# Twelve expert tile pairs moved into the first scan group, with loads that wait for a counted number of scattered columns

## The chip, the cores and the metric

The kernel runs on one core of a Trainium2 chip. Its time is the device time of one execution in microseconds. Engine names in the profile: PE is TensorE (PEld its weight loads), DVE is VectorE, ACT is ScalarE, POOL is GpSimd, SP is the engine whose queue issues most DMAs.

## What is computed

`x` is 2 sequences of 512 tokens with 256 features. Both branches read the layer norm of it, and the output is their sum with `x`:

```python
x = L0_attn_hidden_states
xn = _layernorm(x, axis=-1)
x = x + attn_ref(xn, ...) + ffn_ref(xn, ...)

# attn_ref: a selective state space layer, d_inner 512, d_state 16, dt_rank 128
x, z = split(xn @ in_proj_w.T)
x = silu(causal_conv4(x) + conv_b)
dt, Bm, Cm = split(x @ x_proj_w.T)
dt = softplus(dt @ dt_proj_w.T + 2 * dt_proj_b)
# for each channel d and state n, along the 512 tokens:
h[l] = exp(dt[l] * A[d, n]) * h[l - 1] + dt[l] * Bm[l, n] * x[l]
y = sum_n(h * Cm[:, n]) + x * D
out = (y * z) @ out_proj_w.T

# ffn_ref: 64 experts, each token goes to its 8 most probable ones
probs = softmax(xn @ gate_w.T)
out = sum over the 8 chosen e of probs[e] * ((silu(xn @ g_e.T) * (xn @ u_e.T)) @ w2_e.T)
```

## The kernel before

**Experts.** Routing gives each of the 1024 x 8 choices of an expert a slot. Slots are ordered by expert, each expert filled up to whole tiles of 128. There are 128 tiles, taken as 64 pairs (`PAIRS`). GpSimd writes the rows of the normed x to their slots in DRAM (`slot_x`), with one indirect DMA for each of 8 token tiles `t` and 8 slot columns `k` (L327 to L331); `k8` holds a token's slots with the largest first. For each pair SP loads 256 rows of `slot_x` (`load_x`) and two experts' weights (`load_w`, 2 x 384 KB), and stores the result to `slot_y` (`store_y`). TensorE's `step` for pair p is a pipeline of three: `fetch` transposes x of pair p, `gate_up` works on pair p - 1, `down` on pair p - 2. ScalarE copies x and y out of PSUM (`take_x`, `take_y`) and makes the tanh, VectorE has two operations a pair (`hidden`, L592 and L595). `take_y` waits until the store of two pairs before has landed. At the end GpSimd gathers the rows back by 64 indirect DMAs (L371), and they are weighted by `c8` and added: by TensorE with diagonal matrices (`combine`) for seven token tiles, by VectorE in 8 operations for the last (L697).

**Scan.** The 1024 (sequence, channel) rows are 8 groups of 128 partitions, each with 16 states, 128 scans of 512 tokens. For each state ScalarE makes dA (`decay`), someone makes dbu (`spread_u`), VectorE scans (L572) and multiplies by C (`times_c`, L578), and the products are summed in a PSUM bank by matmuls with the identity. `finish_group` closes a group two states into the next.

**Order.** All of it is written out by hand, each engine with its own program:

- Group 0: VectorE alone makes dbu, in `pair0`; the products go to 16 buffers, so it waits for no sum. GpSimd issues the scatters meanwhile. SP then waits for all scatters and 12 sums before it loads x.
- Groups 1 to 5 (`G1` to before `G2`): scans and expert pairs interleaved, a light group with 12 pairs (`LIGHT`), group 3 (`GH`) heavy with 16, where also the rows of B and C of the second sequence are spread through PSUM. GpSimd makes dbu here (L337) and adds the products in pairs (L344), so TensorE has 8 sums a group.
- Groups 6 and 7 (`G2`, `G3`): `pair0` on VectorE again, with the gathers on GpSimd and `combine` and `project_out` on TensorE.

```python
            sp.wait_ge(scat, 16 * NT * K)
            sp.wait_ge(acc_ok, 3 * PART + C)
            for i in range(4):
                load_x(i, i)
```

## Time and profile before

| | us |
|---|---|
| median of 3 runs | 508.83 (508.74 to 509.46) |
| the profiled execution | 509.57 |
| its span, first to last instruction | 507.4 |
| VectorE busy | 430.5 |
| TensorE busy | 430.4 |
| GpSimd busy | 293.8 |
| ScalarE busy | 246.7 |

The profiled execution took 2.17 us more than its span, and the median of the runs is 0.74 us below it. Busy time is a mean over stages: a stage is best cut where a scan group starts, which is where VectorE's scan reads `dA` and not a PSUM bank (or, in groups that read `dA` throughout, at the first of 16).

### The profile page before, as it was taken

What the parts mean: (1) busy time and instruction counts of PE and PEld (TensorE: products, weight loads), DVE (VectorE), ACT (ScalarE), POOL (GpSimd) and SP (SyncE); (2) the same over time, 40 slices, a digit from 0 to 9 for tenths busy, and PEclk for the clock granted to TensorE, in tenths of its full rate; (3) what the DMA queues carried; (4) which work ended last, traced back from release to release, by engine and by line L of the source; (5) the groups of instructions that cost most, each with busy time, mean ns of one, the idle gap of its engine ahead of it and who ended that gap; (6) DMA issues with size and microseconds to landing.
All of it is one profiled execution on the core that took longest, in us unless ns stands there. A gap on an engine that the chain in (4) does not pass through costs nothing.

```text
span 507.4 us, 9083 instructions
## 1 busy us (share of the span) xinstructions
PE 430.4 (85%) x2136; PEld 304.8 (60%) x2136; DVE 430.5 (85%) x646; ACT 246.7 (49%) x469; POOL 293.8 (58%) x260
## 2 busy tenths in 40 slices
PE   1986969038889999999999997999999949887996
PEld 1732424011157888788787885788878835454754
DVE  5288999989989888898789795888888889999994
ACT  1245367032435655555455665565555632454560
POOL 2000678777756766666545434566766537777772
PEclk9989979655569999999999997999999989997999
DMA  8999399722249999999999997899999944333432
GB/s 278 428 427 424 126 381 398 268 94 103 103 135 310 314 330 348 333 316 314 317 324 312 324 322 268 257 319 326 327 329 331 327 152 122 103 115 106 124 105 88
DMA packets 55417, 132.29 MB, mean 261 GB/s; under 512 B 7616, under 2 KB 11712, under 8 KB 53344
## 3 DMA queue, kind: packets, MB, share of 16 engines
q1 hardware_dynamic: 49248, 115.21, 65.6%
q0 software_dynamic: 6144, 16.79, 10.3%
q8 instruction: 11, 0.18, 0.1%
q14 instruction: 14, 0.11, 0.1%
HBM read 88.39 MB, written 43.58 MB: 260 GB/s over the span
## 4 chain that ended last, share of the span: by engine, by line
SPq 26%; POOL 18%; PE 15%; issue 15%; DVE 12%; DMA 12%; ACT 1%; POOLq 1%; DVEq 0%; ACTq 0%
POOL slot_x L329 13%; SPq L260 10%; SPq L261 6%; DMA slot_x<-bc 5%; DVE bank L572 5%; DMA slot_y<-x_sb 5%; PE bank L1004 4%; SPq L236 4%; SPq L264 3%; SPq L267 3%; PE bank L1015 2%; PE bank L1031 2%; DVE dbu L565 2%; PE bank L974 2%; DVE hc L578 2%
## 5 line engine op out<-in xcount | busy, mean ns | idle before, releaser
L337 POOL TENSOR_TENSOR dbu<-dtu,bc 128x512 f32 x80 | 101.9, 1274 | 99.5 <-DVE bank L572 86.8
L329 POOL DMA_INDIRECT slot_x<-x_sb,slot x64 | 68.8, 1075 | 68.2 <-DMA slot_x<-bc 49.0
L572 DVE TENSOR_TENSOR_SCAN bank<-dA,dbu 128x512 f32<-128x512 f32 x68 | 90.1, 1325 | 10.4 <-POOL dbu L337 1.7
L756 ACT ACTIVATE dA<-dt_sb,a_neg 128x512 f32<-128x512 f32 (+1 forms) x68 | 49.4, 727 | 66.3 <-DVE bank L572 66.1
L572 DVE TENSOR_TENSOR_SCAN bank<-bank,dbu 128x512 f32<-128x512 f32 x60 | 73.8, 1230 | 5.8
L782 ACT COPY x_sb<-bank 128x512 f32<-128x512 f32 x66 | 38.6, 585 | 75.0 <-DMA slot_y<-x_sb 72.7
L1004 PE MATMUL bank<-x_sb,wring 128*128 128x128 f32 x528 | 67.9, 283 | 0.1
L1004 PEld LDWEIGHTS bank<-x_sb,wring 128*128 128x128 f32 x528 | 64.8, 199 | 1.1 <-issue 0.5
L578 DVE TENSOR_TENSOR hc<-bank,bc 128x512 f32<-128x512 f32 x90 | 61.8, 686 | 1.4 <-POOL hp L344 0.3
L756 ACT ACTIVATE bank<-dt_sb,a_neg 128x512 f32 x60 | 41.7, 695 | 9.6 <-DVE bank L572 9.6
L592 DVE SCALAR_TENSOR_TENSOR gt<-th,bank 128x256 f32<-128x256 f32 x65 | 27.0, 416 | 22.5 <-ACT th L776 22.1
L770 ACT COPY x_sb<-bank 128x512 f32<-128x512 f32 x64 | 38.0, 593 | 7.6 <-PE bank L991 7.6
L776 ACT ACTIVATE th<-bank 128x256 f32<-128x256 f32 x65 | 25.2, 388 | 25.4 <-PE bank L1004 24.7
L1015 PE MATMUL bank<-wring,wdt 128*128 128x256 f32 x136 | 35.7, 385 | 1.1 <-ACT x_sb L782 1.0
L974 PE MATMUL bank<-wring,ident 128*128 128x512 f32 x20 | 16.7, 928 | 22.6 <-DVE wring L578 22.6
L344 POOL TENSOR_TENSOR mask<-hc 128x512 f32<-128x512 f32 x21 | 31.2, 1486 | 7.6 <-DVE hc L578 6.4
L595 DVE SCALAR_TENSOR_TENSOR wdt<-gt,bank 128x256 f32<-128x256 f32 x65 | 27.4, 422 | 6.8
L565 DVE TENSOR_TENSOR dbu<-dtu,bc 128x512 f32<-128x512 f32 x48 | 32.4, 674 | 0.5 <-DVEq L559 0.5
L1004 PE MATMUL bank<-x_sb,win 128*128 128x128 f32 x256 | 31.5, 276 | 0.3 <-DMA win<-w_moe 0.3
L1004 PE MATMUL bank<-x_sb,xT 128*128 128x128 f32 x256 | 31.2, 275 | 0.0
L1004 PEld LDWEIGHTS bank<-x_sb,win 128*128 128x128 f32 x256 | 29.9, 192 | 0.5 <-DMA win<-w_moe 0.5
L1004 PEld LDWEIGHTS bank<-x_sb,xT 128*128 128x128 f32 x256 | 29.9, 192 | 0.0
(180 smaller groups left out, 796.5 us busy)
## 6 DMA issues: line engine op xcount, KB each, us to landing
wring<-w_moe SPq DMA_DIRECT2D x64, 384.0 KB, 4.5
slot_y<-x_sb SPq DMA_DIRECT2D x66, 256.0 KB, 4.8
slot_x<-bc SPq DMA_DIRECT2D x16, 1024.0 KB, 22.1
xT<-w_moe SPq DMA_DIRECT2D x32, 384.0 KB, 4.5
win<-w_moe SPq DMA_DIRECT2D x32, 384.0 KB, 4.7
bc<-bc_dram SPq DMA_DIRECT2D x8, 1024.0 KB, 15.9
xg<-slot_x SPq DMA_DIRECT2D x32, 256.0 KB, 4.6
xT<-slot_x SPq DMA_DIRECT2D x16, 256.0 KB, 4.9
```

What stands on the lines that cost most here:

```text
L260: e = sp.value_load(tile_e[0:1, bass.ds(2 * p + j, 1)], min_val=0, max_val=E - 1)
L329: pool.indirect_dma_start(slot_x, bass.IndirectOffsetOnAxis(ap=slot[:, t * K + k:t * K + k + 1], axis=0), x_sb[:, t, :], None).then_inc(sc ...
L337: nc.gpsimd.tensor_tensor(dbu[:, j], at(dtu, g), bc[:, bass.ds(n, 1), 0].rearrange("p a l -> p (a l)"), ALU.mult).then_inc(dbu_ok, 1)
L344: nc.gpsimd.tensor_tensor(hps[j], hc[:, 0], hc[:, 1], ALU.add).then_inc(hp_ok, 1)
L565: nc.vector.tensor_tensor(dbu[:, j], at(dtu, g), bc[:, bass.ds(n, 1), 0].rearrange("p a l -> p (a l)"), ALU.mult).then_inc(dbv_ok, 1)
L572: nc.vector.tensor_tensor_scan(H[:], dA[:, j] if fall is None else fall, dbu[:, j], 0.0, ALU.mult, ALU.add).then_inc(scan_ok, 1)
L578: nc.vector.tensor_tensor(ring[n % len(ring)] if ring else hc[:, j], H[:], bc[:, bass.ds(n, 1), 1].rearrange("p a l -> p (a l)"), ALU.mult ...
L756: nc.scalar.activation(dA[:, j] if fall is None else fall, at(dt_sb, g), ACT.Exp, scale=a_neg[:, bass.ds(g, 1), bass.ds(n, 1)].rearrange(" ...
L770: nc.scalar.copy(xTs[:, i].rearrange("p b d -> p (b d)"), XT[:]).then_inc(xc_ok, 1)
L782: nc.scalar.copy(ysb[:, i].rearrange("p b d -> p (b d)"), YT[:]).then_inc(yc_ok, 1)
L1004: mm = nc.tensor.matmul(GU[1 - i % 2][:, (2 * half + j) * P:(2 * half + j + 1) * P], w_buf[w][:, k * 2 * P + half * P:k * 2 * P + (half + ...
L1015: mm = nc.tensor.matmul(YT[:, j * DM:(j + 1) * DM], hh[:, 2 * (i % 2) + j], w_buf[(2 * i + 4) % 8 + j][:, WGU:], start=True, stop=True)
```

## The change

- Scatters go column by column, lowest slots first (k = 7 first). Each column has a semaphore; GpSimd waits for a column in the middle of the next one and raises `cols_ok`.
- How many columns a pair needs is counted: the smallest slot of each column (`low`, a transpose on TensorE, `lowest`) against the end of the pair (`lim`, `reach`), summed by a matmul to `need`, for the first 16 pairs. SP reads the number and waits for so many columns (`load_early`).
- Group 0 has 12 steps of pairs now. VectorE's `first(n)` has the operations of `hidden` from state 4 on, dbu by VectorE as before. TensorE sums every state by itself (one sum a step, three in step 0). The ring of products is 7 buffers, not 16, and the buffers for x transposed and y no longer lie in `x_sb` but in `wx`/`wgate` (`wxg`) and `wout`.
- Groups 1, 2 light, 3 heavy, 4 light; groups 5, 6 and 7 (`GT` on) are of the last kind. `combine` begins with state 12 of these 48 and does all eight token tiles; VectorE only copies the last two from PSUM.
- `x_sb` is loaded again behind pair 11's loads and not after the last pair; `wout` is loaded after the last store and not after the zeroing.
- ScalarE copies z of groups 4 to 7 ahead of the scans, and its decays run up to five states ahead; GpSimd waits for the sums of group 0 before it makes dbu for group 1.

```diff
-        hc_first = whole + [wdt[:], xg[:, 0].rearrange("p j d -> p (j d)"), xg[:, 1].rearrange("p j d -> p (j d)"),
-                            wx[:].rearrange("p t n -> p (t n)")[:, 0:L]] + [
-            f[:].rearrange("p t e -> p (t e)") for f in (mask, prob, key)] + [hp[:], hc[:, 0], hc[:, 1]]
+        hc_first = [hc[:, 0], hc[:, 1]] + [f[:].rearrange("p t e -> p (t e)") for f in (prob, key)] + [dA[:, 1]] + hps[::-1]
...
+        RING0, AHEAD0, LAST = len(hc_first), 4, 3 * NS
         LIGHT = 3 * QG // 2
-        V_HEAVY, V_LAST = (GH - G1) * LIGHT, (GH - G1) * LIGHT + 2 * QG
-        assert V_LAST + (G2 - GH - 1) * LIGHT == PAIRS
+        V_HEAVY, V_LAST = GH * LIGHT, GH * LIGHT + 2 * QG
+        assert V_LAST + (GT - GH - 1) * LIGHT == PAIRS and NS - AHEAD0 == LIGHT and LIGHT + 4 == EARLY
...
+        PROJ = {8: (4, 0), 10: (5, 0), 20: (4, 1), 22: (5, 1), 24: (6, 0), 26: (7, 0), 28: (6, 1), 30: (7, 1),
+                37: (4, 2), 39: (5, 2), 41: (6, 2), 43: (7, 2)}
+        COMB = 12
...
-            sp.dma_start(wout[:], w_out.rearrange("(t p) n -> p t n", p=P)).then_inc(ld_wout, 16)
...
+            def load_early(p):
+
+                c = sp.value_load(need[0:1, p:p + 1], min_val=1, max_val=K)
+                sp.wait_ge(cols_ok, c)
+                load_x(p, p % 4)
...
-            sp.wait_ge(scat, 16 * NT * K)
-            sp.wait_ge(acc_ok, 3 * PART + C)
-            for i in range(4):
-                load_x(i, i)
+            sp.wait_ge(rt, RT_NEED)
+            sp.wait_ge(c8_ok, NT // 2)
+            for p in range(4):
+                load_early(p)
+            sp.wait_ge(sp_v, SP_STEPS * G)
+
+            for p in range(LIGHT):
+                sp.wait_ge(ye_ok, p + 1 + C)
+                load_w(p + 2, (p + 2) % 4)
+                sp.wait_ge(yc_ok, p + 1 + C)
+                store_y(p, p % 2)
+                sp.wait_ge(t_ok, p + 1)
+                load_early(p + 4)
+            sp.wait_ge(cols_ok, K)
+            sp.dma_start(x_sb[:], x_t).then_inc(ld_res, 16)
...
-            sp.wait_ge(gu_ok, PAIRS + 1 + C)
             for j in range(2):
                 sp.wait_ge(y_st[j], 16 * (PAIRS // 2 + 1) + 16)
-            sp.dma_start(x_sb[:], x_t).then_inc(ld_res, 16)
+            sp.dma_start(wout[:], w_out.rearrange("(t p) n -> p t n", p=P)).then_inc(ld_wout, 16)
...
-            for t in range(NT):
-                for k in range(K):
+
+            def arrived(c):
+
+                pool.wait_ge(scat[c], 16 * NT)
+                pool.sem_inc(cols_ok, 1)
+
+            for c in range(K):
+                k = K - 1 - c
+                for t in range(NT):
+                    if c and t == NT // 2:
+                        arrived(c - 1)
                     pool.indirect_dma_start(
                         slot_x, bass.IndirectOffsetOnAxis(ap=slot[:, t * K + k:t * K + k + 1], axis=0),
-                        x_sb[:, t, :], None).then_inc(scat, 16)
-
+                        x_sb[:, t, :], None).then_inc(scat[c], 16)
+            arrived(K - 1)
+            pool.wait_ge(acc_ok, NS - 2 + C)
...
+            nc.vector.tensor_reduce(low[:], k8[:].rearrange("p t k -> p k t"), AX.X, ALU.min).then_inc(rt, 1)
             dve.wait_ge(pe_r, 5)
             nc.vector.tensor_scalar(tile_e[:], PS[4][0:1, P:P + TILES], float(E - 1), None, ALU.min).then_inc(rt, 1)
-            for d in range(1, DT):
-                conv_block(d)
+            conv_block(1)
+            conv_block(2)
+            dve.wait_ge(pe_r, 6)
+            nc.vector.tensor_reduce(lowest[:], PS[4][0:K, 2 * P:3 * P], AX.X, ALU.min).then_inc(rt, 1)
+            dve.wait_ge(rt, RT_LOWEST)
+            nc.vector.tensor_scalar(reach[:], lim[:], lowest[:], None, ALU.is_ge).then_inc(rt, 1)
+            conv_block(3)
...
+            dve.wait_ge(pe_r, 7)
+            nc.vector.tensor_copy(need[:], PS[4][0:1, 3 * P:3 * P + EARLY]).then_inc(rt, 1)
...
-            for q in range(NS // 4):
-                dve.wait_ge(bc_ld[q], 32)
-                if q == 0:
+                    times_c(g, n, j, hc_end)
+
+            def first(n):
+
+                if n % 4 == 0:
+                    dve.wait_ge(bc_ld[n // 4], 32)
+                if n == 0:
                     spread_u(0, 0, 0)
-                    pair0(0, 0, 0, hc_first)
-                else:
-                    pair0(0, 2 * q - 1, 0, hc_first)
-                    pair0(0, 2 * q, 0, hc_first)
-            pair0(0, QG - 1, 0, hc_first, ())
+                dve.wait_ge(dbv_ok, n + 1)
+                scan(0, n, n % 2, dA_light(n))
+                if n >= AHEAD0:
+                    hidden(n - AHEAD0, n % 2)
+                if n % 4 == 3 and n < NS - 1:
+                    dve.wait_ge(bc_ld[n // 4 + 1], 32)
+                if n < NS - 1:
+                    spread_u(0, n + 1, 1 - n % 2)
+                if n >= RING0:
+                    dve.wait_ge(acc_ok, n - RING0 + 1 + C)
+                times_c(0, n, n % 2, hc_first)
+
+            for n in range(NS):
+                first(n)
...
-            with dve.Fori(GH + 1, G2) as g:
+            with dve.Fori(GH + 1, GT) as g:
                 light(g, (g - GH - 1) * LIGHT + V_LAST)
             hidden(PAIRS, 0)
...
-            spread_u(G2, 0, 0)
-            dve.wait_ge(hp_ok, (G2 - G1) * QG + 1)
+            spread_u(GT, 0, 0)
+            dve.wait_ge(hp_ok, (GT - G1) * QG + 1)
             dve.wait_ge(t_ok, PAIRS)
             dve.wait_ge(ye_ok, PAIRS + 2 + C)
-            pair0(G2, 0, NS, hc_end)
-            finish_group(G2 - 1)
-            for q in range(1, QG - 1):
-                pair0(G2, q, NS, hc_end)
-            pair0(G2, QG - 1, NS, hc_end, (G3,))
-            pair0(G3, 0, 2 * NS, hc_end)
-            finish_group(G2)
-            for q in range(1, QG - 1):
-                pair0(G3, q, 2 * NS, hc_end)
-            pair0(G3, QG - 1, 2 * NS, hc_end, ())
+            for g in range(GT, G):
+                count = (g - GT + 1) * NS
+                pair0(g, 0, count)
+                finish_group(g - 1)
+                for q in range(1, QG - 1):
+                    pair0(g, q, count)
+                pair0(g, QG - 1, count, (g + 1,) if g < G3 else ())
             finish_group(G3)
 
-            t = NT - 1
-            dve.wait_ge(ld_res, 16)
-            dve.wait_ge(g_ld[t % 4], (t // 4 + 1) * 16 * K)
-            for k in range(K):
-                if k:
-                    dve.wait_ge(fin, k)
-                nc.vector.scalar_tensor_tensor(x_sb[:, t], rows[t % 4][:, k], c8[:, t, k:k + 1], x_sb[:, t],
-                                               ALU.mult, ALU.add).then_inc(fin, 1)
-            dve.wait_ge(fin, K)
-            dve.wait_ge(o_ps, 4)
-            nc.vector.tensor_tensor(x_sb[:, t], x_sb[:, t], OUT[t], ALU.add).then_inc(fin, 1)
+            for t in range(NT - 2, NT):
+                dve.wait_ge(o_ps, t - 3)
+                nc.vector.tensor_copy(x_sb[:, t], OUT[t]).then_inc(fin, 1)
...
-
-            for n in range(NS):
-                decay(0, n, n % 2)
-                if 11 <= n < 15:
-                    keep_z(n - 7)
...
-            act.wait_ge(scat, 16 * NT * K)
-            decay(G1, 0, 0)
+            act.wait_ge(z_ok, G)
+            for n in range(AHEAD0 + 1):
+                decay(0, n, n % 2, dA_light(n))
+            for m in range(LIGHT):
+                n = m + AHEAD0
+                take_x(m, m % 2)
+                decay((n + 1) // NS, (n + 1) % NS, (n + 1) % 2, dA_light(n + 1))
+                tanh(m, m % 2)
+                take_y(m, m % 2, m // 2)
...
-            for t in range(NT - 1):
+            for t in range(NT):
...
-            for t in range(4, NT - 1):
+            for s in range(LAST - 2, LAST):
+                decay(GT + s // NS, s % NS, s % 2)
+            for t in range(4, NT - 2):
                 act.wait_ge(o_ps, t - 3)
                 output(t)
...
+            pe.wait_ge(rt, RT_TILE)
+            nc.tensor.transpose(PS[4][0:K, 2 * P:3 * P], low[:], ident[:]).then_inc(pe_r, 1)
...
+                if k == 2:
+                    pe.wait_ge(rt, RT_REACH)
+                    nc.tensor.matmul(PS[4][0:1, 3 * P:3 * P + EARLY], ones[0:K, 0:1], reach[:], start=True, stop=True).then_inc(pe_r, 1)
             pe.wait_ge(ld_wdt, 16)
-            pe.wait_ge(rt, RT_TILE)
+            pe.wait_ge(rt, RT_NEED)
...
+            for m in range(LIGHT):
+                step(m // 4, m % 4)
+                for n in (m + 2,) if m else range(3):
+                    sum_states(0, n, hc_first, 1)
...
-            pe.wait_ge(ld_wout, 16)
-            pe.wait_ge(yz_ok, DT)
             pe.wait_ge(hh_ok, PAIRS + 1 + C)
-            for n in range(NS // 2):
-                sum_states(G2, n, hc_end, PART if n % PART == PART - 1 else 0)
-                if n == 6:
+            for s in range(LAST):
+                n, i = s % NS, s % 4
+                sum_states(GT + s // NS, n, hc_end, PART if n % PART == PART - 1 else 0)
+                if s == 4:
+                    pe.wait_ge(ld_wout, 16)
+                    pe.wait_ge(yz_ok, DT)
+                if s == 10:
                     pe.wait_ge(yc_ok, PAIRS + 2 + C)
-                for k in (n % 2 * 2, n % 2 * 2 + 1):
-                    project_out(n // 2, k)
-            pe.wait_ge(ld_res, 16)
-            for s in range(NS // 2, 2 * NS):
-                n, i = s % NS, s % 4
-                sum_states(G2 + s // NS, n, hc_end, PART if n % PART == PART - 1 else 0)
-                combine(s // 4 - 2, (2 * i, 2 * i + 1))
+                if 4 <= s < COMB:
+                    for k in (s % 2 * 2, s % 2 * 2 + 1):
+                        project_out((s - 4) // 2, k)
+                if s == COMB:
+                    pe.wait_ge(ld_res, 16)
+                if COMB <= s < COMB + 4 * NT:
+                    combine((s - COMB) // 4, (2 * i, 2 * i + 1))
```

## Rows read from the trace of the kernel before

**Rows 1.** The page: the span, and the chain's shares by engine.
```profile
span 507.4 us, 9083 instructions
...
SPq 26%; POOL 18%; PE 15%; issue 15%; DVE 12%; DMA 12%; ACT 1%; POOLq 1%; DVEq 0%; ACTq 0%
```

**Rows 2.** Stretches: busy us and operations of each engine, clock, DMA share, GB/s.
```profile
80.00:90.00 10.00, 9.24 (x22) 3.81 (x20) 9.90 (x17) 8.97 (x15) 7.87 (x8) 1.00 1.05 402
104.00:140.00 36.00, 26.14 (x26) 6.54 (x26) 33.20 (x42) 13.49 (x20) 27.47 (x29) 0.50 0.28 99
148.00:150.00 2.00, 2.00 (x13) 1.66 (x13) 0.68 (x2) 1.20 (x3) 2.00 (x2) 1.00 0.13 48
193.50:240.70 47.20, 45.13 (x304) 38.11 (x304) 40.54 (x59) 26.50 (x52) 31.28 (x25) 1.00 0.96 325
240.70:313.40 72.70, 68.36 (x438) 54.98 (x437) 57.55 (x82) 41.32 (x83) 30.39 (x24) 0.97 0.96 320
360.50:412.00 51.50, 49.78 (x324) 41.31 (x322) 42.24 (x63) 28.79 (x57) 30.03 (x24) 1.00 0.90 305
```

**Rows 3.** Timeline of VectorE, group 0: start, length, operation.
```profile
105.70 1.24 DVE L572 TENSOR_TENSOR_SCAN bank<-dA,dbu 128x512 f32<-128x512 f32 x1 [1.07 <-ACT dA L756]
...
111.94 0.67 DVE L565 TENSOR_TENSOR dbu<-dtu,bc 128x512 f32<-128x512 f32 x1
112.53 0.68 DVE L578 TENSOR_TENSOR wring<-bank,bc 128x512 f32<-128x512 f32 x1
113.34 1.23 DVE L572 TENSOR_TENSOR_SCAN bank<-dA,dbu 128x512 f32<-128x512 f32 x1
...
146.09 1.86 DVE L572 TENSOR_TENSOR_SCAN bank<-dA,dbu 128x512 f32<-128x512 f32 x1
```

**Rows 4.** Timeline of GpSimd: the first and the last of 64 scatters.
```profile
52.74 1.24 POOL L329 DMA_INDIRECT slot_x<-x_sb,slot  x1 [49.03 <-DMA slot_x<-bc]
...
139.77 0.97 POOL L329 DMA_INDIRECT slot_x<-x_sb,slot  x1 [0.30 <-issue]
```

**Rows 5.** Timelines of the end, groups 6 and 7 and what follows.
```profile
411.95 1.23 DVE L572 TENSOR_TENSOR_SCAN bank<-dA,dbu 128x512 f32<-128x512 f32 x1 [1.43 <-PE bank L1015]
...
493.05 1.23 DVE L572 TENSOR_TENSOR_SCAN bank<-dA,dbu 128x512 f32<-128x512 f32 x1
...
497.08 0.69 DVE L586 TENSOR_TENSOR u<-u,xpad 128x512 f32<-128x512 f32 x1
...
497.84 0.95 POOL L371 DMA_INDIRECT dtu<-slot_y,slot_r  x1 [0.30 <-issue]
...
500.84 1.89 PE L1088 MATMUL bank<-wout,u 128*128 128x256 f32 x8
...
504.87 0.42 DVE L701 TENSOR_TENSOR x_sb<-x_sb,bank 128x256 f32<-128x256 f32 x1
```

**Rows 6.** Timeline of VectorE ahead of group 0: the clamp of tile_e.
```profile
43.79 0.27 DVE L472 TENSOR_SCALAR tile_e<-bank 1x128 int32<-1x128 f32 x1
```

**Rows 7.** Timeline of TensorE between the projections: dt (L933) and z (L948).
```profile
61.37 3.67 PE L933 MATMUL bank<-hc,wdt 128*128 128x512 f32 x8
...
70.89 2.04 PE L933 MATMUL bank<-hc,wdt 128*128 128x512 f32 x2 [4.13 <-DVE dt_sb L519]
...
81.35 1.02 PE L933 MATMUL bank<-hc,wdt 128*128 128x512 f32 x2
```

**Rows 8.** Timeline of VectorE, light group: two scans, one pair between.
```profile
157.59 1.23 DVE L572 TENSOR_TENSOR_SCAN bank<-bank,dbu 128x512 f32<-128x512 f32 x1
...
160.40 1.23 DVE L572 TENSOR_TENSOR_SCAN bank<-bank,dbu 128x512 f32<-128x512 f32 x1
```

**Rows 9.** Timeline of TensorE, light group: a step with a sum.
```profile
165.86 0.60 PE L991 MATMUL bank<-ident,xg 128*128 128x128 f32 x4
...
169.81 0.60 PE L991 MATMUL bank<-ident,xT 128*128 128x128 f32 x4
```

**Rows 10.** DMA issues: count, KB each, median us from issue to landing.
```profile
wring<-w_moe SPq DMA_DIRECT2D x64, 384.0 KB, 4.5
```

74 lines of the change are left out of this document (39 added, 35 removed).

## The prediction

> **What bounds the kernel now.** I read the page first, then stretches cut where a scan group starts, then the timelines of VectorE, TensorE and GpSimd, and the issues of DMAs. The page has one core, span 507.4 us, and a chain that passes through every engine [rows 1]: no single engine sets the end, so each stage has to be read by itself. VectorE's timeline and the stretches [rows 2 to 4] give this order:
>
> - 0 to 105.7 us: layer norm, routing, projections, softplus; VectorE is 9.9 of 10 us busy in the stretch 80 to 90 [rows 2].
> - Group 0: its first scan starts at 105.70, the first of group 1 at 146.09 [rows 3], so 40.4 us. One state takes (113.34 - 105.70)/3 = 2.55 us, all of it VectorE. GpSimd scatters meanwhile, 64 issues from 52.74 to 139.77, 1.38 us each [rows 4], and the pairs of tiles wait for the last.
> - Groups 1 to 5 with 64 pairs: 146.09 to 411.95 [rows 3, 5], 265.9 us. A light group has 12 pairs and takes 47.2 (193.5 to 240.7), the heavy one with 16 takes 72.7, the last light one 51.5 with the emptying of the pipeline. TensorE is busy 45.1 of 47.2 and 68.4 of 72.7, VectorE 40.5 and 57.6 [rows 2]. TensorE is nearest to full, and the DMA engines are 0.96 busy.
> - Groups 6 and 7: from 411.95 to the last scan at 493.05 [rows 5]; with its own 2.54 that is 83.6, or 41.8 a group, VectorE alone.
> - The end: the gathers, 85.9 us behind the scan at 411.95, issue the last at 497.84. VectorE's last operation starts at 504.87 [rows 5] and the span ends at 507.4.
>
> So 105.7 + 40.4 + 265.9 + 83.6 + 11.8 = 507.4. The change shifts 12 pairs from a middle group, where GpSimd makes dbu, into group 0, where VectorE makes it, and so turns a middle group into a third pure scan group. That is the whole bargain, and each part of it has a price.
>
> **Ahead of group 0.** Added on VectorE: two small reductions, one compare, one copy. The nearest row is the clamp of tile_e, 0.27 us [rows 6]; four of such size with some waiting between them are 0.8. VectorE is full here, so they lie on the path. The copy of `need` brings a new wait as well: TensorE used to project dt for the first groups at 61.37, now it waits for that copy, which stands behind the six picks and weighings on VectorE, at about 67. It has been idle for 7 us then. From 67.2 on all 8 projections of dt and 4 of z stand in front of the last dt: 32 matmuls of 0.43 (3.67 for eight in a row at 61.37, the lag of the last one's end included) are 13.8 us, so 81.0 at the full clock. Its first matmuls after a gap ran at half speed before too (2.04 us for two at 70.89); 3 us of that make it 82.5, twice that 84. Before, the last dt projection ended at 82.4 [rows 7], so the end is 0 to 1.6 later, and 5 if the clock stays low. I take 0.5. Together 1.3; bounds 0.3 (hidden in waits) and 5. The transpose and the small matmul on TensorE lie in its idle time. Without wout the SP queue is only lighter: nothing, since the 16 zeroing DMAs in front of it stay.
>
> **Group 0 after.** VectorE's floor first. A light state with one pair's two operations lasts 160.40 - 157.59 = 2.81 us [rows 8], without dbu; spreading adds 0.59 (111.94 to 112.53, [rows 3]). So 4 states of 2.55 and 12 of 3.40: 51.0 us. TensorE next: a step with a sum behind it takes 169.81 - 165.86 = 3.95 [rows 9], and each of the 12 steps has one now (light groups: 8 of 12). Step 0 carries sums of states 0, 1 and 2, so step 1 can't begin before state 2 is multiplied: 2 x 2.55 + 1.7, then the last sum, 2.04 at the half clock; with the semaphores between that is about 9 us behind the first scan. The granted clock was 0.50 from 104 to 140 with TensorE 26.1 of 36 us busy, and 1.00 in the stretch 148:150, some 3 us after pairs had begun [rows 2]; so step 1 costs about 1.5 us more. Then 11 x 3.95 = 43.4. Of the last step, its down projection and sum (4 matmuls of 0.43, 1.7) lie behind what VectorE waits for, and tanh, the two operations and the product (about 2.2) come behind that. 9 + 1.5 + 43.4 + 0.5 = 54.4. TensorE and not VectorE sets group 0, if data comes.
>
> Does it come? A pair moves 768 KB of weights, 256 of x, 256 of y: 1.31 MB, at 3.95 us 332 GB/s. The scatters beside them move 99 GB/s until 141 us, at a DMA share of 0.28; a light group has 0.96 at 325 GB/s; and 80 to 90 us, where loads of bc and scatters ran together, shows 402 GB/s at 1.05 [rows 2]. Two ends. If bytes count and 402 can be had again, 303 are left for pairs: 4.3 us each over the 26 us from step 1 to the last scatter, so 6.0 pairs for 6.6, some 2.4 us late, and the lead of the loads takes that up. The lead: weights go out when a step's down projection ends and are wanted two steps, a sum and a fetch later, 9.3 us; 1.5 for issuing and 4.5 to land [rows 10] leave about 3. If shares add, 0.68 is left, 325 x 0.68/0.96 = 230 GB/s, 5.7 us a pair: 4.6 pairs for 6.6, 8 us late, less 3, so 5. I take 1.5: group 0 lasts 56 us, 15.6 more than before; ends 51.0 and 64 (TensorE and DMA lagging together).
>
> The Trainium skill bears on this ("DMA: Bandwidth & Descriptors", section on issuing engines): DMAs from SP and GpSimd run on the same 16 engines and interleave, so scatters take from the pairs' share. By that rule in its strict form the 5 us end would hold and the span would be 3.5 us above my sum. The rows do not settle it, since the highest shares stand beside different rates.
>
> **The waits on columns.** Columns go out from the lowest slot up, 8 scatters of 1.38 us each, and a column is signalled 4 issues behind its last. Counting how many columns reach into each pair on the reference's inputs (seed 0) gives 1, 2, 3, 4, 4, 4, 4, 5, 5, 6, 6, 6, 6, 6, 7, 7 for pairs 0 to 15. Columns 4, 5, 6, 7 are then signalled at about 102, 113, 124 and 135 us [rows 4]. Load 7 (5 columns) is asked for in step 3, near 127; load 9 (6) in step 5, near 135; load 14 (7) in step 10, near 154. All are past. Behind a waiting load on SP stand the weights of the next pair, so a missed column would stop all, but each has 10 us. SP issues the same DMAs a pair as before. GpSimd now waits for all sums before it spreads for group 1; by then its scatters are done. Price nothing.
>
> **The middle.** One light group goes: -47.2, since the emptying at the end stays and what starts the pairs is in group 0 now. Bounds: -44 (12 steps of TensorE's work) and -51.5. The 1 MB load of x_sb moves in here: 1.05 MB at 325 GB/s is 3.2 us of DMA. It was hidden behind groups 6 and 7. TensorE is what is fullest, and the last middle stretch has only 0.90 of DMA share [rows 2], so I take 1.0, ends 0 and 3.2.
>
> **The end.** A third pure group: +41.8. The gathers need 85.9 us of now 125.4, so they end 40 us early, and combining fits too (a state brings TensorE 4 matmuls of a combine, 2 of a sum and 2 of a projection, 8 like those at 500.84 that took 1.89 us [rows 5] or a little longer, in 2.55). wout lands while the first states run. VectorE's product ends at 497.77 (497.08 + 0.69); its last operation was at 504.87, behind the last gather and eight multiply-adds. Now four projections (500.84, the same 1.89 us), a semaphore and a copy stand there: last operation 2.3 behind 497.77 for 7.1, so -4.8. Bounds -3.5 and -5.5.
>
> **Sum:** 1.3 + 15.6 + 1.0 - 47.2 + 41.8 - 4.8 = +7.7; span 515.1. The profiled run took 509.57, 2.17 above its span, and the median of the runs is 0.74 under it: 515.1 + 1.43 = 516.5 us.
>
> **Rivals.** (A) The forecast, 516.5, own range 513 to 520: chance 0.56. (B) DMA shares add up in group 0 and step waits pile up: 5 in place of 1.5, and the same backlog makes x_sb cost its 3.2 in group 1: 516.5 + 3.5 + 2.2 = 522.2. For it: 0.28 + 0.96. Against: scatters and loads together have moved 402 GB/s, more than a light group's 325. The Trainium skill's rule above is this case. Chance 0.22. (C) TensorE keeps up with VectorE, its floor of 51.0 holds, preparing is 0.3 and x_sb is hidden: 507.4 + 10.6 + 0.3 - 10.2 = 508.1, time 509.5, no change. Against: 12 steps of 3.95 are 47.4 and can't begin at the first scan. Chance 0.09. (D) Faster: the heavy group falls to the light pace. Its 16 pairs take 4.54 each against 3.95 [rows 2, 9]; if what stretches it is a shortage of loads (share 0.96) that the earlier start relieves, 72.7 goes to 63, so 516.5 - 9.7 = 506.8. It decides from 64.0 us for that group on down. Against: TensorE is busy 68.4 of the 72.7, with the rows of B and C in it. Chance 0.07. (E) The clock falls back to 0.50 in the gaps of group 0, again and again: five times 1.5 us, 524.0. TensorE at 73% busy stayed at 0.50 there. Chance 0.06.
>
> **Numbers.** A measurement of this kernel tells some 0.2% (1 us) from no change. Slower: A, B, E, 0.84. Same: C, 0.09. Faster: D, 0.07. The range 510.2 to 524.0 holds A and B and leaves out C and D.
>
> **What would show it.** First scan of group 1 some 56 us behind the first of group 0; if 51, C; if over 60 with weights as releaser, B. Window of group 0: DMA share over 0.9, clock near 1.0 after its first fifth. Group 5's first scan near 383; three groups of 41.8; last operation 2.3 us behind the last product; gathers over by 470. No wait on SP for a column. Wrong I would be if TensorE's step in group 0 were shorter than 3.95, if the heavy group's length moved, or if stores landed so late under load that ScalarE, which waits for them before it copies y, fell behind TensorE.

## The result, and the profile after

| | before | after |
|---|---|---|
| median on one chip, us | 509.07 (508.74 to 509.46, 4 runs) | 522.75 (521.22 to 522.86, 4 runs) |
| profiled execution | 509.57 | 522.86 |
| its span | 507.4 | 519.9 |

The ratio is 1.0261, interval 1.0241 to 1.0282: slower by 13.7 us. The forecast was 516.5, slower, so the sign is right, the range of 510.2 to 524.0 holds the time, and the size of the change was put too low: 7.4 us against 13.7. Ratios, here and below, are taken over the undisturbed runs of both kernels on one chip, while medians are over all runs, so a ratio need not be the quotient of two medians.

From the page of the kernel after, the busy times, three rows of the 40 slices, and the chain of waits:

```profile
span 519.9 us, 8828 instructions
...
PE 436.4 (84%) x2173; PEld 311.4 (60%) x2173; DVE 436.6 (84%) x659; ACT 248.6 (48%) x476; POOL 264.5 (51%) x237
...
PEclk9988979579999999999999999899996998997998
DMA  8999299957999999999999999979934333342001
GB/s 282 429 427 380 86 376 400 313 172 256 364 348 321 363 310 340 320 311 353 323 326 315 337 325 289 309 230 316 346 143 121 107 105 103 102 122 71 0 0 40
...
DVE 40%; SPq 25%; PE 14%; issue 12%; DMA 4%; ACT 2%; POOL 2%; DVEq 1%; POOLq 0%; ACTq 0%
```

Still no engine sets the end alone [rows 1]. The DMA row shows what moved: 0.7 or more in all slices from 9 to 28, counted from 0, and then eight slices of 0.2 to 0.4, in which three groups without pairs go by. The stretches cut at the scan groups (columns: length; busy us and instructions of PE, PEld, DVE, ACT, POOL; granted clock; DMA share; GB/s) are group 0, two parts of it, group 1, the heavy group 3, and groups 5 to 7:

```profile
108.28:165.72 57.44, 52.80 (x326) 42.68 (x326) 47.82 (x72) 27.29 (x53) 28.66 (x28) 0.98 0.87 300
118.00:128.00 10.00, 8.60 (x58) 7.15 (x57) 9.29 (x16) 6.04 (x12) 7.69 (x8) 1.00 0.75 250
128.00:138.00 10.00, 10.00 (x65) 8.30 (x64) 8.92 (x15) 4.75 (x10) 7.86 (x8) 1.00 1.01 352
165.72:215.54 49.82, 45.24 (x296) 37.67 (x297) 41.34 (x58) 25.74 (x51) 32.16 (x25) 1.00 0.96 336
263.36:335.36 72.00, 67.33 (x438) 54.89 (x437) 57.48 (x83) 41.36 (x83) 30.30 (x24) 0.98 0.97 316
386.45:509.80 123.35, 98.25 (x293) 57.42 (x293) 117.06 (x148) 53.40 (x115) 65.68 (x64) 0.92 0.27 79
```

In group 0 TensorE is busy 52.8 of 57.4 us, VectorE 47.8: TensorE is the fuller one, as said, and its clock is full (it was 0.50 in group 0 before [rows 2]). From 128 to 138 scatters and pairs together move 352 GB/s at a share of 1.01: the DMA engines are full. Scatters alone moved 99 GB/s before [rows 2]; if they still do, some 250 are left for the pairs (an estimate from these two figures), nearer to the 230 of adding shares than to the 303 of counting bytes. The lag stays small all the same, because this lasts only until the scatters end near 143; from 118 to 128 the share is 0.75.

Laid beside the prediction's sum:

| stretch | predicted | measured | off |
|---|---|---|---|
| to the first scan (before: 105.70) | +1.3 | 108.28, +2.6 | 1.3 |
| group 0 | 56 | 57.4 | 1.4 |
| groups 1 to 4 with the pairs | 219.7 | 220.7 | 1.0 |
| groups 5 to 7 | 125.4 | 125.9 | 0.5 |
| behind them | 7.0 | 7.6 | 0.6 |
| span | 515.1 | 519.9 | 4.8 |
| median above span | 1.43 | 2.85 | 1.4 |

The 219.7 are 265.9 - 47.2 + 1.0; the 7.0 are 11.8 - 4.8. All six rows are short, each by a little, and none the other way. The places where this shows are next.

**Ahead of group 0.** TensorE (first two lines) and VectorE (the rest) of the kernel after; a number in brackets is the idle time before an instruction and what ended it:

```profile
67.64 6.21 PE L985 MATMUL bank<-hc,wdt 128*128 128x512 f32 x8 [4.19 <-DVE need L539]
83.13 1.02 PE L985 MATMUL bank<-hc,wdt 128*128 128x512 f32 x2
```

```profile
43.79 0.26 DVE L506 TENSOR_REDUCE low<-k 128x8 f32<-128x64 f32 x1
43.97 0.27 DVE L508 TENSOR_SCALAR tile_e<-bank 1x128 int32<-1x128 f32 x1
...
51.82 0.27 DVE L512 TENSOR_REDUCE lowest<-bank 8x1 f32<-8x128 f32 x1
52.13 0.22 DVE L514 TENSOR_SCALAR reach<-lim,lowest 8x16 f32<-8x16 f32 x1
...
67.39 0.15 DVE L539 CAST need<-bank 1x16 int32<-1x16 f32 x1
...
73.03 0.75 DVE L562 TENSOR_SCALAR dt_sb<-bank,dtb 128x512 f32<-128x512 f32 x1 [1.64 <-ACT dA L782]
```

The four added operations are small, 0.15 to 0.27 us each; together they shift VectorE's first operation on dt from 69.99 to 70.64, 0.65 us. Then comes what was priced too low: the projection that the copy releases starts after 4.19 us without work on TensorE and takes 6.21 us for eight, at a granted clock of 0.58 from 67.6 to 73.7, where it took 3.67 [rows 7]. VectorE runs dry at its second dt, 1.64 us, because ScalarE had the projected dt late. The last projection ends 1.8 us later than before.

**Group 0 and its end.** ScalarE's copies of y, TensorE in the steps, and the handover to group 1, VectorE and GpSimd, in the kernel after:

```profile
139.85 0.59 ACT L821 COPY wout<-bank 128x512 f32<-128x512 f32 x1 [2.80 <-DMA slot_y<-wout]
...
148.96 0.59 ACT L821 COPY wout<-bank 128x512 f32<-128x512 f32 x1 [3.01 <-DMA slot_y<-wout]
```

```profile
137.33 1.02 PE L1026 MATMUL bank<-hc,ident 128*128 128x512 f32 x2
...
141.52 1.02 PE L1026 MATMUL bank<-hc,ident 128*128 128x512 f32 x2
...
145.65 1.02 PE L1026 MATMUL bank<-prob,ident 128*128 128x512 f32 x2
...
148.28 1.16 PE L1053 MATMUL bank<-wxg,wring 128*128 128x128 f32 x8 [0.28 <-DMA wring<-w_moe]
149.69 1.10 PE L1064 MATMUL bank<-wring,wdt 128*128 128x256 f32 x4 [0.24 <-ACT wout L821]
150.62 1.02 PE L1026 MATMUL bank<-key,ident 128*128 128x512 f32 x2
```

```profile
163.22 0.68 DVE L621 TENSOR_TENSOR hc<-bank,bc 128x512 f32<-128x512 f32 x1
165.72 2.06 DVE L615 TENSOR_TENSOR_SCAN bank<-dA,dbu 128x512 f32<-128x512 f32 x1 [1.82 <-POOL dbu L372]
```

```profile
142.50 0.96 POOL L363 DMA_INDIRECT slot_x<-x_sb,slot  x1 [0.31 <-issue]
164.20 2.49 POOL L372 TENSOR_TENSOR dbu<-dtu,bc 128x512 f32 x2 [20.74 <-PE bank L1026]
```

Steps last 3.95 us, except the three between 137.33 and 150.62: 4.19, 4.13 and 4.97, together 1.4 us over. There the last scatters are going (the last is issued at 142.50), and ScalarE waits 2.80, 2.16 and 3.01 us for stores of y before it copies the next y. The weights were late once, by 0.28 us. So the lag seems to come more by way of the stores than of the loads. And at the end VectorE waits 1.82 us for GpSimd, which had stood idle for 20.74 us at the wait for all sums that the change gave it.

### The profile page after: what moved, and what is told of

It reads as the page before. It is cut to its first block, busy times and chain, and to the rows that moved or that the text cites. A ratio compares the mean times of both kernels' runs of the same rounds, so it can differ in the third digit from the quotient of the medians.

```text
span 519.9 us, 8828 instructions
## 1 busy us (share of the span) xinstructions
PE 436.4 (84%) x2173; PEld 311.4 (60%) x2173; DVE 436.6 (84%) x659; ACT 248.6 (48%) x476; POOL 264.5 (51%) x237
## 4 chain that ended last, share of the span: by engine, by line
DVE 40%; SPq 25%; PE 14%; issue 12%; DMA 4%; ACT 2%; POOL 2%; DVEq 1%; POOLq 0%; ACTq 0%
DVE bank L615 14%; SPq L267 11%; SPq L268 6%; DVE dbu L608 5%; PE bank L1053 3%; SPq L271 3%; DMA slot_y<-wout 3%; SPq L274 3%; DVE u L419 2%; PE bank L1064 2%; DVE hc L621 2%; PE bank L1026 2%; DVE xg L621 1%; PE bank L926 1%; PE bank L1080 1%
## 5 line engine op out<-in xcount | busy, mean ns | idle before, releaser
L372 POOL TENSOR_TENSOR dbu<-dtu,bc 128x512 f32 (+1 forms) x64 | 81.5, 1274 | 102.0 <-DVE bank L615 68.9
L821 ACT COPY wout<-bank 128x512 f32<-128x512 f32 x66 | 38.7, 586 | 89.7 <-DMA slot_y<-wout 86.0
L1053 PE MATMUL bank<-wxg,wring 128*128 128x128 f32 x528 | 68.3, 283 | 4.9 <-DVEq L602 3.2
L1053 PEld LDWEIGHTS bank<-wxg,wring 128*128 128x128 f32 x528 | 64.6, 198 | 6.8 <-DVEq L602 3.6
L800 ACT ACTIVATE bank<-dt_sb,a_neg 128x512 f32<-128x512 f32 (+1 forms) x60 | 41.8, 696 | 13.1 <-DVE bank L615 13.1
L809 ACT COPY wxg<-bank 128x512 f32<-128x512 f32 x64 | 37.9, 593 | 6.5 <-PE bank L1040 6.4
L1053 PE MATMUL bank<-wxg,win 128*128 128x128 f32 x256 | 31.4, 276 | 0.0
L1053 PE MATMUL bank<-wxg,xT 128*128 128x128 f32 x256 | 31.2, 275 | 0.0
L1053 PEld LDWEIGHTS bank<-wxg,win 128*128 128x128 f32 x256 | 29.9, 192 | 0.1
L1053 PEld LDWEIGHTS bank<-wxg,xT 128*128 128x128 f32 x256 | 29.8, 192 | 0.0
```

Of the source, the lines that this page charges most:

```text
L372: nc.gpsimd.tensor_tensor(dbu[:, j], at(dtu, g), bc[:, bass.ds(n, 1), 0].rearrange("p a l -> p (a l)"), ALU.mult).then_inc(dbu_ok, 1)
L800: nc.scalar.activation(dA[:, j] if fall is None else fall, at(dt_sb, g), ACT.Exp, scale=a_neg[:, bass.ds(g, 1), bass.ds(n, 1)].rearrange(" ...
L809: nc.scalar.copy(xTs[:, i].rearrange("p b d -> p (b d)"), XT[:]).then_inc(xc_ok, 1)
L821: nc.scalar.copy(ysb[:, i].rearrange("p b d -> p (b d)"), YT[:]).then_inc(yc_ok, 1)
L1053: mm = nc.tensor.matmul(GU[1 - i % 2][:, (2 * half + j) * P:(2 * half + j + 1) * P], w_buf[w][:, k * 2 * P + half * P:k * 2 * P + (half + ...
```

## The experiments

Each kernel is the changed one with one edit, or with several where it says so. Two of the chips, one of them only for a time, ran all kernels, the one before too, slower and less evenly, and there the variants show stops at instruction issue (idle time that nothing in the profile explains); only groups without such a stop are read against the 57.4. Four things were to be settled: which engine holds group 0 (T1 and T4 below are two theories of it; the labels start anew with each expectation), whether the scatters delay the pairs, what the wait for `need` costs, and what GpSimd's wait costs.

**Half the scatters.** The last four columns in the order of issue (k = 3 to 0) are not scattered, and their count is signalled at once, so those rows of `slot_x` stay as they were zeroed:

```diff
-            for c in range(K):
+            for c in range(K // 2):
...
-            arrived(K - 1)
+            arrived(K // 2 - 1)
+            pool.sem_inc(cols_ok, K // 2)
```

> The changed kernel with the scatters of the last four columns left out (rows of those columns stay zero, so the expert part of the output lacks them); the count of columns is still raised to eight. No scatter runs beside group 0 then. Theory T1, TensorE's step of 3.95 us sets group 0: from the first scan of group 0 to the first of group 1 it stays near 57.4 us, 1 to 2 shorter, since only the three long steps between 138 and 151 us (together 1.4 us over 3.95 each) go. Theory T2, the scatters take DMA time that the pairs lack: 4 us shorter or more. Time 520.5 to 522 by T1, 519 or less by T2.

> The changed kernel without the scatters of the last four columns, once more, since the first chip stalled at the issue of instructions in the kernel before as well. T1, TensorE's step sets group 0: 1 to 2 us shorter than 57.4, ratio to before 1.022 to 1.026. T2, scatters take DMA time that the pairs lack: 4 us or more shorter, ratio 1.018 or less.

First run (before 538.79 on this chip): 537.99, ratio 1.005 (0.99 to 1.02), group 0 from 119.51 to 175.50, 56.0 us. Second, on an even chip (before 510.27): 520.07, ratio 1.015 (1.006 to 1.024), group 0 from 108.41 to 164.39, 55.98 us, and every step of TensorE 3.95. VectorE's two scans at the ends of it in the second run:

```profile
108.41 1.23 DVE L616 TENSOR_TENSOR_SCAN bank<-dA,dbu 128x512 f32<-128x512 f32 x1 [1.06 <-ACT dA L801]
164.39 2.07 DVE L616 TENSOR_TENSOR_SCAN bank<-dA,dbu 128x512 f32<-128x512 f32 x1 [1.95 <-POOL dbu L373]
```

So the scatters beside the pairs cost 1.5 us of group 0 against the kernel after, the prediction's 1.5, and rival B, which wanted 5, fell. GpSimd's wait stays (1.95). The 1.5 is no constant: in two runs below, where the first scan comes 2.9 us earlier and the last scatter is issued at the same time (142.9 and 142.5), the steps lose 2.6 and 3.0 us.

**Half the sums.** TensorE leaves out the sums of the odd states 1 to 13 of group 0, so y of that group lacks them. The edit does one thing more: GpSimd waits for the count of state 13, which is now raised without a sum, so GpSimd starts its products for group 1 earlier.

```diff
+                    if n % 2:
+                        pe.wait_ge(hc_ok, n + C + 1)
+                        pe.sem_inc(acc_ok, 1)
+                    else:
                         sum_states(0, n, hc_first, 1)
```

> The changed kernel with TensorE's sums of the odd states 1 to 13 of group 0 left out (the output of group 0's channels lacks these states); the counter is raised all the same. From step 1 on six sums of 0.86 us are gone. T1: TensorE sets group 0, so it shortens by up to 5.2 us, down to VectorE's floor of 51.0 plus the wait for GpSimd at the end (1.8): 57.4 to 52.5 or 53.5, time 518 to 519. T2 (loads) or a rival T3, that VectorE and ScalarE set the pace: under 1.5 us.

> The changed kernel without TensorE's sums of states 1, 3, ..., 13 of group 0, once more. T1: group 0 shortens from 57.4 to 52.5 to 53.5 us, six sums of 0.86 less, held up by VectorE's floor of 51.0 and the 1.8 us of GpSimd; ratio 1.017 to 1.020. If loads (T2) or VectorE (T3) set the pace, under 1.5 us shorter, ratio 1.024 or more.

First: 560.8, ratio 1.062 (1.051 to 1.073), group 0 63.6 us behind stops at issue, not to be read. Second: 520.11, ratio 1.016 (1.008 to 1.025), group 0 from 108.75 to 164.77, 56.02. VectorE and GpSimd at the end of it in the second run:

```profile
164.05 0.69 DVE L621 TENSOR_TENSOR hc<-bank,bc 128x512 f32<-128x512 f32 x1
164.77 1.52 DVE L615 TENSOR_TENSOR_SCAN bank<-dA,dbu 128x512 f32<-128x512 f32 x1
```

```profile
162.69 2.51 POOL L372 TENSOR_TENSOR dbu<-dtu,bc 128x512 f32 x2 [20.31 <-DVE bank L615]
```

VectorE no longer waits for GpSimd there. Its last product of group 0 ends 56.0 us after the first scan, in the kernel after 55.6. So 5 us less of sums (6 x 0.86) shortened nothing; the 1.4 us are the 1.8 of GpSimd's wait less 0.4 of longer waits in the steps. VectorE runs at its own pace until 140 us, and then loses 5.1 us in five waits for tanh, behind ScalarE's waits of up to 4.06 us for stores. TensorE alone as the limit of group 0 fell.

**Both at once.** Only the two edits together:

> The changed kernel with both: no scatters of the last four columns and no TensorE sums of states 1, 3, ..., 13 of group 0. Either alone took 1.4 to 1.5 us off group 0's 57.4. T4, two limits of nearly the same height, TensorE's step of 3.95 us and the flow of loads beside the scatters: both together take off more than the two alone add up to, 4 to 5 us, so group 0 lasts 52.5 to 53.5. Rival T5, the loads alone are the limit even without scatters (a light group already has a DMA share of 0.96 at 3.95 us a pair): it stays at 55 to 56.

526.6, ratio 1.0015 (0.997 to 1.006; before 526.68 on this chip). Group 0 from 109.99 to 163.86, no stop in it: 53.87, 3.6 shorter than 57.4, where each edit alone gave 1.5 and 1.4. That looks like T4, but GpSimd's wait is gone here too. Counted to the end of VectorE's last product of group 0, us:

| kernel | first scan | product ends | between | then waits for GpSimd |
|---|---|---|---|---|
| after | 108.28 | 163.90 | 55.6 | 1.82 |
| half the scatters | 108.41 | 162.44 | 54.0 | 1.95 |
| half the sums | 108.75 | 164.74 | 56.0 | 0 |
| both | 109.99 | 163.83 | 53.8 | 0 |
| GpSimd early (below) | 105.39 | 162.66 | 57.3 | 0 |
| three repairs (below) | 105.47 | 163.10 | 57.6 | 0 |

The scatters give 1.6 without the edit of the sums and 2.2 with it, half the sums nothing with all scatters and 0.2 with half of them. So 3.6 is the scatters and GpSimd's wait, and T4's "more than the two alone add up to" isn't shown. With the 1.95 added back, both together would be 55.8 (an estimate), inside T5's 55 to 56: with fewer sums, the pairs' own loads and stores hold the group even without scatters. ScalarE and a stretch of this run, in which no scatter is issued after 95.08:

```profile
152.34 0.59 ACT L822 COPY wout<-bank 128x512 f32<-128x512 f32 x1 [2.77 <-DMA slot_y<-wout]
```

```profile
148.00:158.00 10.00, 9.46 (x59) 7.79 (x58) 8.15 (x12) 5.47 (x12) 0.00 (x0) 1.00 0.95 308
```

TensorE's step of 3.95 and the flow of the pairs' data lie at nearly the same height: without the scatters each step is 3.95, and with fewer sums on top the stores hold ScalarE. VectorE's floor of 51.0 is 2.9 away still.

**The copy of need earlier.** It moves from behind the six picks and weighings to behind the first picking, so that TensorE may project dt sooner:

```diff
                 weigh(t)
+                if t == 0:
+                    dve.wait_ge(pe_r, 7)
+                    nc.vector.tensor_copy(need[:], PS[4][0:1, 3 * P:3 * P + EARLY]).then_inc(rt, 1)
```

> The changed kernel with the copy of need on VectorE moved from behind the third picking of weights to behind the first, some 7.5 us earlier, so that TensorE's projections of dt are released before it has stood idle and fallen to the half clock. T1 for the preparation: the wait for need is what puts the first scan at 108.28 and not at 106.5 (eight matmuls took 6.21 us at 67.64 where they had taken 3.67); the first scan comes back to about 106.5, 1.5 to 2 us earlier, time near 521. Rival: the 2.6 us are the added operations and waits on VectorE itself: the scan stays within 0.5 us of 108.3.

> The changed kernel with only the copy of need moved from behind the third picking to behind the first, once more. First scan at 106.5 (T1: it is TensorE's late and half-clock start on dt) or within 0.5 us of 108.3 (rival: the added operations themselves). Everything behind it is shifted by the same; ratio 1.023 by T1.

**The load of x_sb behind the last stores,** where group 1 doesn't have it; the copy of `need` is where the change put it, so the kernel is also the other half of the comparison:

```diff
             sp.wait_ge(cols_ok, K)
-            sp.dma_start(x_sb[:], x_t).then_inc(ld_res, 16)
...
             sp.dma_start(wout[:], w_out.rearrange("(t p) n -> p t n", p=P)).then_inc(ld_wout, 16)
+            sp.dma_start(x_sb[:], x_t).then_inc(ld_res, 16)
```

> The changed kernel with the 1 MB load of x_sb behind the last store, where it was before. The predicted price of having it in the middle was 1.0 us, bounds 0 and 3.2. Group 1 (49.8 us with it) should last 47.5 to 49, groups 2 to 4 as they are, ratio 1.022 to 1.025. If group 1 stays at 49.8, its length comes from the backlog of group 0 and not from this load.

Need early: 556.25, ratio 1.056 (1.047 to 1.064), and on another chip 551.58, 1.051 (1.046 to 1.056). x_sb late: 550.6, 1.050 (1.044 to 1.056), on that other chip. The times say nothing here, since stops at issue lengthened group 0 of all three to between 80.8 and 83.4 us. The stretch ahead of it can be read. The starts of `tile_e` on VectorE and of the first scan (a run's `tile_e` comes at 41 to 42 or at 44, whatever the kernel, so the difference is given), and how long the copy of `need` itself waits:

| kernel | tile_e | first scan | between | copy waits |
|---|---|---|---|---|
| before | 43.79 | 105.70 | 61.9 | no copy |
| after | 43.97 | 108.28 | 64.3 | 0 |
| half the scatters, second run | 43.91 | 108.41 | 64.5 | 0 |
| half the sums, second run | 44.35 | 108.75 | 64.4 | 0 |
| x_sb late (need as in after) | 41.99 | 106.14 | 64.2 | 0 |
| GpSimd's products early (as in after; below) | 41.20 | 105.39 | 64.2 | 0 |
| need early, first run | 40.98 | 104.74 | 63.8 | 1.40 |
| need early, second run | 41.49 | 106.08 | 64.6 | 2.16 |
| three repairs (need early; below) | 41.25 | 105.47 | 64.2 | 1.79 |
| dbu of the last group on GpSimd (need early; below) | 44.06 | 106.44 | 62.4 | 0 |

Where `tile_e` comes at 41, the copy's place makes no difference. VectorE shows why, in the kernel with three repairs:

```profile
58.99 0.16 DVE L546 CAST need<-bank 1x16 int32<-1x16 f32 x1 [1.79 <-PE bank L985]
```

With the early copy TensorE projects at 62.47, eight in 3.67, at full clock, and VectorE's second dt doesn't wait. But now the copy itself waits, 1.79 us for the small matmul that counts, which stands behind projections on TensorE. The 1.64 us moved to another place. Where `tile_e` comes at 44, as in the profile of the kernel after, VectorE reaches the copy later and the count is there. VectorE and TensorE in the last kernel of the table:

```profile
59.94 0.15 DVE L549 CAST need<-bank 1x16 int32<-1x16 f32 x1
```

```profile
61.76 3.67 PE L1001 MATMUL bank<-hc,wdt 128*128 128x512 f32 x8
```

The first scan is at 106.44, 1.9 us sooner after `tile_e` than in the kernel after and 0.5 later than before. That is T1's 106.5: with a late `tile_e` the wait for `need` is what costs, about 1.9 of the 2.4 us, and the added operations the rest. It is one profile, and it shows the late case alone. Placed between (behind the second or fourth operation of picking) the copy might cost neither; that wasn't tried.

The load of x_sb costs next to nothing: from the finish of group 0 to that of group 1 it is 47.25 us without the load and 47.63 with it (need early), same chip, and 46.77 with it on the other chip. My 1.0 was generous, rival B's 3.2 far off. All three are after a group 0 with stops, in which loads and stores could catch up. Without such stops the same stretch takes 48.2 to 50.9 us, the 50.9 without the load (three repairs). So what group 1 takes over its 46.6 of before fits a backlog from group 0 and not this load; that too is argued, since no run lifts the backlog alone.

**GpSimd's first products ahead of its wait.**

```diff
             arrived(K - 1)
-            pool.wait_ge(acc_ok, NS - 2 + C)
...
+            for i in range(2):
+                for j in range(2):
+                    spread_u(G1, 2 * i + j, j)
+                if i == 0:
+                    pool.wait_ge(acc_ok, NS - 2 + C)
+                add_pair(i - 1, 1 - i)
```

> The changed kernel with GpSimd's wait for the sums of group 0 moved behind its first two products for group 1, to where it writes the first buffer that those sums read. T1: the first scan of group 1 stood 1.8 us still for GpSimd; that wait goes, group 0 lasts 55.6 us in place of 57.4, time near 521. Rival: TensorE's step is late anyway and the 1.8 us are lost again at the first tanh of group 1: the time stays within 0.5 us of 522.75.

> GpSimd makes the first two products of group 1 before it waits for TensorE's sums of group 0; nothing else is changed. T1 (at the handover from group 0 to group 1 VectorE waits for GpSimd's dbu, which stood 1.8 us behind the wait for the sums): the wait of the first scan of group 1 for GpSimd's dbu (1.82 us in the changed kernel) is gone, group 0 lasts 55.5 to 56 us where no instruction stall lies in it, time 520.5 to 521.5. T2 (TensorE's last step with its sum ends late in any case, and the wait for GpSimd only hides it): the 1.8 us come back as a wait for TensorE's bank or for t_ok in the next state or two, group 1 starts 1.8 us earlier but its own length grows by as much, 522.7.

First: 558.14, ratio 1.049 (1.033 to 1.066), group 0 65.7 us behind stops at issue, not to be read. Second: 520.95 (517.3 to 523.4), before 511.84, ratio 1.019 (1.011 to 1.026), an even profile. The wait is gone, but group 0 runs from 105.39 to 162.69, 57.3 us, as long as with it. ScalarE and TensorE of the second run:

```profile
154.86 0.58 ACT L828 COPY wout<-bank 128x512 f32<-128x512 f32 x1 [2.86 <-DMA slot_y<-wout]
```

```profile
151.70 1.02 PE L1033 MATMUL bank<-dA,ident 128*128 128x512 f32 x2
...
156.53 1.02 PE L1033 MATMUL bank<-mask,ident 128*128 128x512 f32 x2
...
160.78 1.02 PE L1033 MATMUL bank<-hp,ident 128*128 128x512 f32 x2
```

Steps of 4.83 and 4.25 stand here, late in the group, with the stores late again. In the kernel after, those last steps were 3.95. Five steps of this run are over 3.95, by 2.6 us in all against 1.4. The handover itself did get shorter: from the end of TensorE's last step to the first scan of group 1 it is 1.05 us (161.64 to 162.69), in the kernel after 2.39 (163.33 to 165.72). The longer steps took it back. The edit can't reach them, since it acts only at the end of the group; but the first scan is 2.9 us earlier here and the last scatter isn't (142.88), so more of the group lies beside scatters. That fits, and is not shown. From the first scan to the finish of group 1 both take about the same: 220.06 - 105.39 = 114.7 and 222.60 - 108.28 = 114.3. The 1.8 us were not won.

**Three repairs together** (need early, GpSimd early, x_sb late):

> The three repairs together: the copy of need behind the first picking, GpSimd's two products ahead of its wait for the sums, the 1 MB load of x_sb behind the last stores in place of group 1. T1 (each pays what the traces gave it by itself): first scan 2 us earlier (106.2), group 0 1.8 shorter, group 1 0.4 to 1.0 shorter: some 4.5 us, 518.0 (518.5 by the lower figures), still slower than before by 1.8%. T2 (they overlap with the data lag of group 0, so the pairs are waited for whatever starts earlier): 520.5 to 521.5. Either way the kernel before stays the fastest.

518.51 (516.5 to 520.3), ratio 1.016 (1.010 to 1.021), beside 520.95 for GpSimd early alone on the same chip; the two overlap. 518 was T1's number, but not for its reasons: the first scan comes no sooner than in the kernel with GpSimd early, and group 0 lasts 57.7, with 3.0 us lost in the steps. From finish to finish group 1 is even longer, 50.9 against 50.3, group 2 shorter, 47.0 against 48.7, and the heavy one 69.5 against 71.7. Why those two shrink is open.

**With the dbu of the last group on GpSimd too.** The three repairs and one edit more. GpSimd has nothing to do there once the gathers are over, so it makes the products from state 2 of group 7 on:

```diff
-                    dve.wait_ge(dbv_ok, count + n + 1)
+                    if g == G3 and n >= OWN:
+                        dve.wait_ge(dbu_ok, (GT - G1) * NS + n - OWN + 1)
+                    else:
+                        dve.wait_ge(dbv_ok, count + n + 1)
```

> The changed kernel with four edits, each read in a stretch of its own: need copied behind the first picking (first scan at 106.5 in place of 108.28); GpSimd's wait for the sums behind its first two products (group 0 at 55.6 in place of 57.4); x_sb loaded behind the last store again (group 1 at 48 in place of 49.8); and GpSimd, idle once the gathers are out, makes dbu for states 2 to 15 of group 7 (a state from 2.54 to some 2.05, since VectorE's own part is 1.95 and TensorE's 2.15: the last group 6 to 7 us shorter). Sum -11, span near 509, time near 511, which would be the kernel before within 0.5%. If the bargain of groups and not these four waits were wrongly understood, one of the four stretches would not move.

552.61, ratio 1.053 (1.048 to 1.058; before 526.68), group 0 78.4 us with stops. Of the four stretches, the first scan came at 106.44 (106.5 expected, above), group 0 can't be read, and group 1 lasts 46.8 (48 expected, after a group 0 with stops). VectorE in group 7:

```profile
502.81 2.28 DVE L626 TENSOR_TENSOR_SCAN bank<-dA,dbu 128x512 f32<-128x512 f32 x1 [2.51 <-POOL dbu L372]
505.13 0.69 DVE L632 TENSOR_TENSOR xg<-bank,bc 128x512 f32<-128x512 f32 x1
505.95 1.68 DVE L626 TENSOR_TENSOR_SCAN bank<-dA,dbu 128x512 f32<-128x512 f32 x1
...
508.49 1.68 DVE L626 TENSOR_TENSOR_SCAN bank<-dA,dbu 128x512 f32<-128x512 f32 x1
```

A state still lasts 2.54 us. VectorE lost an operation of 0.59 and its scan grew from 1.23 to 1.68 while GpSimd worked beside it; the handover costs 2.51 once on top. For this stretch the expectation missed.

Of all these, none that does the whole work beats the kernel before.

## Why the prediction was right, and where it fell short

**The bargain: right.** A light middle group is swapped for a third one without pairs, and group 0 pays for the pairs. Groups 5 to 7 run at 2.54 us a state, 386.45, 428.27 and 470.51 being starts of scans 41.8 and 42.2 apart; 41.8 was the term. The last gather is issued at 474.05, said to be over by 470; group 5 began 3.5 us later than forecast.

**Group 0: right but for 1.4 us.** The sum was 9 to step 1, 1.5 for its clock, 43.4 for eleven steps, 1.5 of lag and 0.5 at the end. TensorE in step 1:

```profile
116.79 0.60 PE L1040 MATMUL bank<-ident,xg 128*128 128x128 f32 x4
117.22 1.95 PE L1053 MATMUL bank<-wxg,xT 128*128 128x128 f32 x16
120.57 1.13 PE L1064 MATMUL bank<-wring,wdt 128*128 128x256 f32 x4 [1.40 <-DVE wdt L638]
```

Step 1 begins 8.5 us after the first scan. It takes 1.7 more than 3.95, but not for the clock, which is full there (16 matmuls in 1.95, as in later steps): TensorE waits 1.40 us for VectorE's `hidden`. That term had the right size by luck. The eleven steps are 43.4, the lag 1.4, and from the end of the last step to the scan of group 1 it is 2.4 in place of 0.5. So what failed is the step at the end of the part on columns: "GpSimd now waits for all sums before it spreads for group 1; by then its scatters are done. Price nothing." The scatters were done, but the sums were what was late, and the last one is TensorE's, which the same text made the slowest. VectorE waited 1.82 us. Taking that wait away shortened the handover by 1.3 us and not the group, because the steps lost as much more in that run.

"TensorE and not VectorE sets group 0, if data comes" holds only with its condition. Half the scatters brought 1.5 us; half the sums brought nothing but GpSimd's earlier start. The steps are 3.95 where data comes, and fewer sums don't make the group shorter, since the stores and loads of the pairs then hold it.

**Ahead of group 0: the term that was furthest off,** +1.3 against +2.6. The operations were priced well (0.8; they shifted VectorE by 0.65). The error is the 0.5 for the late dt, which is 1.9 by the run with the early copy at the same `tile_e`. I worked out when the last projection ends, 0 to 1.6 later (it was 1.8), and took the lower part, as though only the last one counted. VectorE needs the first ones one by one and ran dry at the second, at 73.03. It is the mechanism named there, the low clock after a gap, mis-sized. The gap was put at 7 us; from 61.37 to 67.2, the text's own times, it would be 5.8, and it was 4.19, since TensorE's work before it ended later.

**Waits on columns: nothing, right.** In the view of waits, SP's own in the kernel after, a single wait of 2.0 us is put down to GpSimd, which signals the columns. It lies ahead of group 0, among the first loads of x, and step 1 of TensorE later waits for VectorE, so it costs nothing:

```profile
SPq L274 <- ACT wout L821: 14.8, 5, 5.4
...
SPq L271 <- POOLq L356: 2.0, 1, 2.0
```

Columns are us in total, times, and the longest. The 14.8 us above it are the stores of y waiting for ScalarE.

**The middle:** 1.0 us more than the sum. It isn't spread over the groups: group 1 lasts 49.8 against 47.4 before, group 2 47.8 against 47.2, the heavy one 72.0 against 72.7 and the last light one 51.1 against 51.5. So group 1 alone is 2.4 over, where 1.0 was set for x_sb. The load is not the cause (0.4 or nothing); a backlog fits better, as said above.

**The end:** 0.5 over in the scans and 0.6 behind them. The last sum ran mostly at the low clock (0.57 granted from 509.7 to 513.6):

```profile
509.80 1.23 DVE L615 TENSOR_TENSOR_SCAN bank<-dA,dbu 128x512 f32<-128x512 f32 x1
...
513.62 0.75 DVE L627 SCALAR_TENSOR_TENSOR u<-u,d_col,bank 128x512 f32<-128x512 f32 x1 [1.86 <-PE bank L1026]
...
516.75 0.86 DVE L743 COPY x_sb<-bank 128x256 f32<-128x256 f32 x2 [1.65 <-PE bank L1141]
```

The last sum took 1.68 us for two matmuls that take 1.02 at full clock. In the kernel with three repairs it took 1.10 and the wait is 1.28 us, but there the last eight projections took 3.58 us at a granted clock of 0.53, against 1.99 here. With combining done early, TensorE has little work in the last states, so some of the very matmuls that end the chain run at the low clock.

**The rivals.** B gave 522.2, nearer to 522.75 than my 516.5, and is still not what happened: it wanted 5 us of lag and 3.2 for x_sb, and 1.4 and at most 0.4 were measured. Full DMA engines it had right. C fell with TensorE's 3.95. D fell, the heavy group took 72.0. E fell, the clock in group 0 was 0.98. Forecast A had a range of its own, 513 to 520, which misses the time by 2.8 us: small shortfalls, all the same way, since I took the lower part of the bounds each time (0.5 of 0 to 5, nothing for a new wait, before's distance of median and span).
